# Gathering the table rows of a graph attention layer by item, straight into place, instead of by tile through a ring

## What is computed

```python
k = _decomp(node_feat, node_type, w_comp_k, w_basis_k).reshape(n, H, DK)
q = _decomp(node_feat, node_type, w_comp_q, w_basis_q).reshape(n, H, DK)
v = _decomp(node_feat, node_type, w_comp_v, w_basis_v).reshape(n, H, DK)
kt = jnp.einsum('nhi,thij->tnhj', k, relation_att)[edge_type, src]
e = (q[dst] * kt).sum(-1) * relation_pri[edge_type] * scale
m = jax.ops.segment_max(e, dst, num_segments=n)
ex = jnp.exp(e - m[dst])
denom = jax.ops.segment_sum(ex, dst, num_segments=n)
a = ex / denom[dst]
vt = jnp.einsum('nhi,thij->tnhj', v, relation_msg)[edge_type, src]
agg = jax.ops.segment_sum(a[..., None] * vt, dst, num_segments=n)
out = _decomp(agg.reshape(n, DH), node_type, w_comp_a, w_basis_a)
out = jax.nn.relu(out + node_feat @ loop_weight + bias)
x = _layernorm(x + out)
```

## Time and profile before

| what | value |
|---|---|
| median of 3 runs | 1298.87 us (1296.42 to 1303.16) |
| the profiled execution: span from its first to its last instruction | 1757.2 us |
| its own time apart from the span | not recorded |
| mean granted TensorE clock | 0.783 of full |
| PE busy | 1160.7 us, 66% |
| DVE busy | 986.6 us, 56% |
| ACT busy | 785.6 us, 45% |
| POOL busy | 881.5 us, 50% |
| DMA, mean over the span | 176 GB/s |

### The profile page before, as it was taken

The page is one execution under the profiler, slowest core; times in us unless marked ns, Lnnn a source line. Parts: engine busy times, 40 slices in busy tenths (PEclk is TensorE's granted clock), DMA queues, the critical chain, the costliest instruction groups (busy, mean ns, idle before and its releaser), DMA issues.

```text
span 1757.2 us, 31429 instructions
## 1 busy us (share of the span) xinstructions
PE 1160.7 (66%) x6730; PEld 962.9 (55%) x6730; DVE 986.6 (56%) x2832; ACT 785.6 (45%) x2217; POOL 881.5 (50%) x915
## 2 busy tenths in 40 slices
PE   8989875657556565566566655566565666656698
PEld 5445434656545554455455554565455565545587
DVE  7877463555445555445555554455554566545677
ACT  4667454444434434443344343443444354434324
POOL 2775354555555554545454545455545554545233
PEclk9999997777677767876777667766777687777699
DMA  8878754555555555545455555555555555555675
GB/s 261 323 289 316 284 172 140 157 148 158 152 159 153 157 151 151 149 141 151 150 163 148 158 152 154 148 160 164 151 162 154 154 168 148 155 150 162 187 242 194
DMA packets 225149, 309.08 MB, mean 176 GB/s; under 512 B 32423, under 2 KB 191119, under 8 KB 217781
## 3 DMA queue, kind: packets, MB, share of 16 engines
q1 hardware_dynamic: 159996, 188.75, 30.6%
q0 software_dynamic: 38880, 106.25, 23.4%
q10 hardware_dynamic: 26088, 12.08, 2.4%
HBM read 139.52 MB, written 58.78 MB: 113 GB/s over the span
## 4 chain that ended last, share of the span: by engine, by line
SPq 34%; issue 31%; PE 12%; DVE 9%; another core or an unknown queue 7%; DMA 2%; DVEq 2%; ACT 1%; POOL 1%; POOLq 0%; ACTq 0%
SPq L1173 27%; PE pb L1900 4%; SPq L1152 2%; PE pb L1923 2%; DVE agg L845 2%; SPq L481 2%; SPq L1170 2%; DVEq L814 2%; DMA kv<-ring 2%; PE pb L2084 1%; SPq L1168 1%; PE pb L2190 1%; PE pb L2028 1%; DVE kv L541 1%
## 5 line engine op out<-in xcount | busy, mean ns | idle before, releaser
L1458 POOL DMA_INDIRECT ring<-table,rows_idx x782 | 745.8, 954 | 736.6 <-SPq L1168 452.5
L2084 PE MATMUL pb<-work,onehot 128*128 128x136 f32 x1664 | 367.5, 358 | 214.1 <-DVE agg L845 152.8
L845 DVE TENSOR_TENSOR agg<-agg,pb 128x136 f32 x832 | 241.8, 291 | 459.9 <-remote 291.8
L2084 PEld LDWEIGHTS pb<-work,onehot 128*128 128x128 f32 x1664 | 307.0, 254 | 242.0 <-issue 210.9
L1650 ACT ACTIVATE work<-pb 128x512 f32<-128x512 f32 x208 | 124.0, 596 | 549.6 <-remote 376.2
L2028 PE MATMUL pb<-q_all,work 128*128 x1664 | 301.0, 340 | 1.3 <-issue 0.8
L2028 PEld LDWEIGHTS pb<-q_all,work 128*128 128x128 f32 x1664 | 280.6, 253 | 7.6 <-issue 4.9
L1637 ACT ACTIVATE work<-lane,neg_lane 128x128 f32<-128x128 f32 x800 | 253.3, 390 | 0.6
L2012 PE MATMUL pb<-ident,onehot 128*128 128x128 f32 x832 | 174.5, 347 | 115.6 <-issue 60.2
L2012 PEld LDWEIGHTS pb<-ident,onehot 128*128 128x128 f32 x832 | 125.4, 180 | 136.0 <-issue 71.3
L686 DVE TENSOR_TENSOR kv<-kv,pb 128x512 f32<-128x512 f32 x208 | 141.5, 680 | 96.6 <-issue 41.7
(11 more groups left out here) (239 smaller groups left out, 1237.2 us busy)
## 6 DMA issues: line engine op xcount, KB each, us to landing
kv<-ring SPq DMA_DIRECT2D x832, 128.0 KB
table<-kv SPq DMA_DIRECT2D x49, 1024.0 KB, 5.2
ring<-table,rows_idx POOLq DMA_INDIRECT x782
kv<-base_rows SPq DMA_DIRECT2D x7, 448.0 KB, 7.6
kv<-in_x_dram SPq DMA_DIRECT2D x8, 384.0 KB, 5.8
seg<-item_bias ACTq DMA_DIRECT2D x48, 64.0 KB
base_rows<-pair ACTq DMA_DIRECT2D x24, 128.0 KB
onehot<-coef_rows SPq DMA_DIRECT2D x3, 1024.0 KB, 5.5
```

The costliest lines, as they stand in the source:

```text
L845: v.tensor_tensor(a, a, PB[banks[i // 2 % len(banks)]][:, (i % 2) * 256:(i % 2) * 256 + W], ALU.add).then_inc(s_added, 1)
L1458: pool.indirect_dma_start(out=ring[:, o:o + 2 * D], out_offset=None, in_=table, in_offset=bass.IndirectOffsetOnAxis(ap=rows_idx[:, t:t + 1 ...
L2084: mm = t_.matmul(PB[banks[k % len(banks)]][:, u * 256:u * 256 + W], onehot[:, o:o + P], wv[:, b % WR, h * 2 + u, :], start=True, stop=True)
```

## The change

The row numbers are laid out by item. They are made early on GpSimd, between the pair products of the set-up, stored by tile in a new DRAM tensor `tile_src`, and gathered by item (seven small indirect DMAs, 512 B rows). TensorE and VectorE then turn and copy 128 columns instead of 112; the last two turns stand at blocks 38 and 39 instead of 37 and 38. `rows_idx` has a column for each item.

In the groups GpSimd alone brings the rows: for each batch it waits until the batch two groups back is weighted and until the batch two before has landed, and issues four gathers from `table` straight into `kv`, 832 in all. The ring, its counts, the 832 copies by SyncE, the tile numbers in `itile` and GpSimd's register loads are gone. SyncE keeps its loads and stores of stages one and three. A smaller buffer `spare` serves stage three where the ring did.

```diff
@@ GpSimd, set-up @@
             for k in range(IPR):
                 did(g_.tensor_scalar(pair[:, 0:TILES], tstart, item_no[:, k:k + 1], None, ALU.is_le))
                 g_.tensor_tensor(pair[:, TILES:2 * TILES], pair[:, 0:TILES], tgap, ALU.mult)\
                     .then_inc(s_pair_made, 1)
+                if k == 1:
+                    pool.wait_ge(s_tile_more, 16 * 4)
+                    did(g_.tensor_copy(srcf, tsrc))
+                if k == 3:
+                    did(g_.tensor_copy(etf, tedge))
+                if k == 5:
+                    did(g_.tensor_scalar(srcf, srcf, float(T), None, ALU.mult))
+            did(g_.tensor_tensor(srcf, srcf, etf, ALU.add))
+            pool.dma_start(tile_src.rearrange("(p c) e -> p c e", c=TPR), srcf.rearrange("p (c e) -> p c e", c=TPR))\
+                .then_inc(s_tile_src, 16)
...
-            pool.wait_ge(s_tile_more, 16 * 4)
-            did(g_.tensor_copy(srcf, tsrc))
-            did(g_.tensor_copy(etf, tedge))
-            did(g_.tensor_scalar(srcf, srcf, float(T), None, ALU.mult))
-            g_.tensor_tensor(srcf, srcf, etf, ALU.add).then_inc(s_lanes_rows, 1)
+            pool.wait_ge(s_tile_src, 16)
             pool.wait_ge(s_item_keys, 32)
             pool.dma_start(krow, item_keys.rearrange("(a k) i -> a k i", a=1)).then_inc(s_item_keys, 16)
+            for k in range(IPR):
+                pool.indirect_dma_start(
+                    out=item_src[:, k, :], out_offset=None, in_=tile_src,
+                    in_offset=bass.IndirectOffsetOnAxis(ap=ic[:, 0, k:k + 1], axis=0)).then_inc(s_item_src, 16)
@@ GpSimd, groups @@
-            def landed(t):
-                pool.wait_ge(s_tile[t % TSEMS], t // TSEMS * 16 + 16)
-                pool.sem_inc(s_landed, 1)
-
-            for t in range(REAL):
-                if t >= AHEAD:
-                    landed(t - AHEAD)
-                if t >= RING and t % 2 == 0:
-                    (done,) = nc.values_load_multi_w_load_instructions(
-                        next_start[0:1, t + 1 - RING:t + 2 - RING], engines=(pool.engine,), min_val=1,
-                        max_val=GROUPS * G, skip_runtime_bounds_check_because="counted from tiles")[1]
-                    pool.wait_ge(s_freed, done & 1023)
-                    hold_apart(pool)
-                o = t % RING * 2 * D
-                pool.indirect_dma_start(
-                    out=ring[:, o:o + 2 * D], out_offset=None, in_=table,
-                    in_offset=bass.IndirectOffsetOnAxis(ap=rows_idx[:, t:t + 1], axis=0))\
-                    .then_inc(s_tile[t % TSEMS], 16)
-            for t in range(REAL - AHEAD, REAL):
-                landed(t)
+            def bring(n):
+
+                g, b = n // NBATCH, n % NBATCH
+                par = g % 2
+                after(pool, s_weighted, g - 2, NBATCH, b + 1)
+                if n >= 2:
+                    pool.wait_ge(s_gathered[(n - 2) // NBATCH % 2][(n - 2) % NBATCH],
+                                 (n - 2) // (2 * NBATCH) * 64 + 64)
+                for u in range(4):
+                    o = (par * G + b * 4 + u) * 2 * D
+                    pool.indirect_dma_start(
+                        out=kv[:, o:o + 2 * D], out_offset=None, in_=table,
+                        in_offset=bass.IndirectOffsetOnAxis(
+                            ap=rows_idx[:, 4 * n + u:4 * n + u + 1], axis=0))\
+                        .then_inc(s_gathered[par][b], 16)
+
+            for n in range(GROUPS * NBATCH):
+                bring(n)
@@ SyncE: `bring` and its loops go, the two loads of stage three stay @@
+            sp.wait_ge(s_weighted, (GROUPS - 2) * NBATCH + 4)
+            sp.wait_ge(s_base_stored, 16 * (GROUPS - 4))
+            load_base(0)
+            sp.wait_ge(s_item_sums, (GROUPS - 2) * 2 * NBATCH + HALF * NB // 2)
+            load_coefs(0, 0, HALF)
```

More of the change, by code:

```diff
@@ L86, in graph_transformer_layer @@
     WORK = 4 * P + 2 * 4 * P + WR * 4 * W + 2 * IH * P + 3 * IH * P
[L88 to L92, removed]
+    assert GROUPS * G < ITEMS
     table = nc.dram_tensor("table", [NP * T, 2 * D], f32, kind="Internal").ap()
@@ L129, in graph_transformer_layer @@
         neg_lane = sb("neg_lane", [P, ITEMS])
-        rows_idx = sb("rows_idx", [P, TILES], i32)
-        strip = sb("strip", [97, ITEMS])
+        rows_idx = sb("rows_idx", [P, ITEMS], i32)
+        strip = sb("strip", [33, ITEMS])
         carries = strip[0:1, :]
[L135 to L138, removed]
+        iblk = strip[32:33, :].bitcast(i32)
         band = sb("band", [33, 3 * ITEMS // 2])
@@ L144, in graph_transformer_layer @@
         kv = sb("kv", [P, 2 * G * 2 * D])
-        ring = sb("ring", [P, RING * 2 * D])
+        spare = sb("spare", [P, CN + 4 * NB * P])
         onehot = sb("onehot", [P, 2 * G * P])
@@ L217, in graph_transformer_layer @@
         tsrc, tedge = [a0.take(TPR * P, TROWS).bitcast(i32) for _ in range(2)]
+        srcf, etf = [a0.take(TPR * P, TROWS) for _ in range(2)]
         a0.at = at
@@ L242, in graph_transformer_layer @@
         y = [s3.take(CN) for _ in range(2)]
-        yo = (s3.take(CN), ring[:, 0:CN])
+        yo = (s3.take(CN), spare[:, 0:CN])
         an = [s3.take(CN) for _ in range(2)]
@@ L258, in graph_transformer_layer @@
         even_coefs = take_coefs(q3, CB)
-        ring_coefs = take_coefs(Space(ring, RING * 2 * D, at=CN), HALF)
+        spare_coefs = take_coefs(Space(spare, CN + 4 * NB * P, at=CN), HALF)
         first_coefs, odd_coefs = take_coefs(h3, HALF), take_coefs(h3, HALF)
@@ L291, in graph_transformer_layer @@
         s_item_starts = sem("s_item_starts")
-        s_lanes_rows = sem("s_lanes_rows")
+        s_lanes = sem("s_lanes")
+        s_tile_src = sem("s_tile_src")
+        s_item_src = sem("s_item_src")
         s_stage0 = sem("s_stage0")
@@ L320, in graph_transformer_layer @@
         s_q_terms = sem("s_q_terms")
-        s_tile = [sem(f"s_tile{r}") for r in range(TSEMS)]
-        s_landed = sem("s_landed")
-        s_freed = sem("s_freed")
         s_segments = [sem(f"s_segments{r}") for r in range(2)]
@@ L426, in coef_of @@
             if ch == 1 and c0 < HALF:
-                return ring_coefs[:, c0:c1, :, :]
+                return spare_coefs[:, c0:c1, :, :]
             if ch % 2:
@@ L1149, in _ @@
                         .then_inc(s_segments[g], 16)
[L1151 to L1178, removed]
             def load_base(ch):
@@ L1877, in turn_items @@
                 if i == 0:
-                    pe.wait_ge(s_lanes_rows, 1)
+                    pe.wait_ge(s_lanes, IPR)
+                if i == 2:
+                    pe.wait_ge(s_item_src, 16 * IPR)
                 bank_free()
-                many = (P, TROWS)[a]
-                each = (lanes, srcf.rearrange("p (c e) -> p c e", c=TPR))[a]
+                each = (lanes, item_src)[a]
                 for k in range(k0, k1):
-                    t_.transpose(PB[0][:, (k - k0) * P:(k - k0) * P + many], each[:, k, :],
-                                 ident[0:many, 0:many]).then_inc(s_items_turned, 1)
+                    t_.transpose(PB[0][:, (k - k0) * P:(k - k0 + 1) * P], each[:, k, :],
+                                 ident[:, :]).then_inc(s_items_turned, 1)
                 bank0.append((s_items_copied, a * IPR + k1))
@@ L1997, in _ @@
             query_products(CHUNKS - 1, 0)
-            pe.wait_ge(s_item_blocks, 48)
+            pe.wait_ge(s_item_blocks, 32)
             L = IH * P
```

21 lines of the change are left out of this document (8 added, 13 removed).

## The result

| | before | after |
|---|---|---|
| median, us (lowest to highest, runs) | 1300.06 (1296.42 to 1303.16, 4) | 1334.51 (1333.71 to 1336.44, 4) |
| ratio after/before, 95% interval | | 1.0269 (1.0240 to 1.0299) |
| forecast | | 1357 (1325 to 1380) |

Slower, as forecast, and inside the range, but 22 us faster than the number.

The account below looks back on a forecast made before the run. The prediction took GpSimd's gathers to bound the groups, with SyncE's copies beside them. It summed 1298.9 + 62.7 for 50 more gathers − 4.5 for the copies = 1357 us, range 1325 to 1380.

Parts of the forecast that it names:

- The freezes: Profile of before: stretches where engines stood still, 452.5 us of GpSimd waiting for SyncE, taken to belong to the recording alone.
- 782 become 832 … +62.7: GpSimd's gathers: 50 more, since tiles spanning blocks are gathered per item, at 1.254 us spacing, +62.7 us, all on the path.
- GpSimd's gathers bound the groups, and SyncE's copies run beside them: Groups of before: 5.0 us a batch for gathering against 4.1 for SyncE's copies, which were taken as hidden.
- Copies … −4.5 us: SyncE's 832 copies go; all but those of the last tiles were taken as hidden behind gathers: −4.5 us.
- The 17.7 missing … I carry them over: Remainder of 1281.2 us summed against 1298.9, put down to time around the span and a start hold in both kernels.
- Start: GpSimd's first wait for weighting against the old hold at the coefficient rows: −0.4, taken as 0, bounded by −10 and +10.
- New waits on GpSimd: Waits for batch n−2 landed and batch n−16 weighted: nothing in the steady state.
- Compute: Compute in the groups needs 4.1 us a batch against 5.0 for gathering, so it follows the gathers closely.
- Landing: A gather's rows land at most 3.4 us after it ends; the new wait allows 6.3 us from its start.
- the late-landing rival: Scattered 1 KB rows land later than 6.3 us after their gather's start; with 7.3 us, +103, 1460 us; chance 0.04.
- The first: Rival: gathers really cost 0.954 us, the ring's hand-over between SyncE and GpSimd bound before; 1230 us after; chance 0.10.
- The second: Rival: compute bound the kernel before at 4.43 us a batch, so the time stays at 1299 us; chance 0.06.

Follow-up runs that it names:

- experiment 4: The kernel after with 52 more gathers into a spare buffer, one behind every fourth batch: 1397.98 us, ratio 1.0719.
- experiment 10: The kernel before with SyncE's wait for the batch before's landing ahead of its second copy instead of its third: 1448.96 us, ratio 1.1085.
- experiment 1: The kernel before, unchanged, recorded a second time: span 1297.0 us, its own time 1299.16 us.
- experiment 9: The kernel before with SyncE's wait for the batch before's landing ahead of its fourth copy instead of its third: 1286.69 us, ratio 0.9848.
- experiment 2: The kernel before with SyncE bringing 16 batches instead of 12 before it stops for the coefficient rows: 1301.3 us, ratio 0.9986.
- experiment 7: The kernel after with only two of each batch's four gathers from the third group on, other places keeping stale rows: 1192.84 us, ratio 0.9142.
- experiment 3: The kernel before with a tile counted landed after four gathers instead of seven: 1350.33 us, ratio 1.0354.

## Why the prediction was right or wrong

**The freezes** belong to the recording: right, and shown now (1297.0 against 1757.2 us).

**"782 become 832 … +62.7"**: right. 50 × 1.2585 = 62.9, and 48 fewer and 52 more gathers moved the time by 1.21 and 1.22 us each, good to about 0.1. The 0.30 behind each gather is real time: by the busy 0.954 alone experiment 4 would have cost 49.6 us, not 63.5. The rule of the Trainium skill (Perfetto Trace Analysis, GPSIMD Engine Instruction), start-to-start spacing instead of the span, agrees with this kernel.

**"GpSimd's gathers bound the groups, and SyncE's copies run beside them"**: the first half held in the mean (4.72 of 4.75 us a batch), the second half failed. It priced SyncE by what it issues, 4.1 us a batch, and left out that L1168 waits in each batch for the landing of the batch before's last copy. With it the rounds shown are 4.52 to 5.39 us, about as long as four gathers, and experiment 10 shows that a longer round sets the time. The landings were in my rows, but as the price of the last tiles alone.

**"Copies … −4.5 us"**: mis-sized. What went with the ring was 5.7 us of holds in the gathers and 15.4 of the tail. Of the tail, 2.2 went with the moved wait (19.9 in experiment 1, 17.7 in experiment 9). The other 13.2 are 8.3 of the longer way through the ring and 6.4 of the shared tiles near the end, less 1.5 by which compute was slower after; how the 8.3 divide into round and count is not shown. I had priced none of it: I added a landing of 3.4 and the copies, 7.9 us in all, where 19.9 stood, and took compute to be ahead of the gathers up to the end.

**"The 17.7 missing … I carry them over"**: wrong, and the larger part of the miss. Only 1.7 to 2.2 us lie around the span and the start hold is nothing (experiment 2). A remainder of a sum that should close is a term not found; it was the round and the tail (8.0 of first to last gather and 12.0 of the tail over my terms, less 4.2 at the start), and most of it went with the change. That the result still lies in the range is partly luck: the lower end, 1325, let the 17.7 go together with a hold at the start, and experiment 2 shows no such hold.

**Start**: forecast 0 within 10. The first gather came 4.1 us earlier than in experiment 1; the recordings with the set-up of before have 194.1 to 196.4, those with the set-up of after 190.8 to 193.5, so about 3. The changed set-up was a small gain, which I had called nothing. Which of its steps gave it is not shown.

**New waits on GpSimd**: right. 4.0 us for weighted batches, 0.9 for landings. **Compute** 4.1 a batch: 4.16 in the mean, but 4.96 in the last group. **Landing** at most 3.4: 2.8 in the median, but 3.8 at most by the view of L1416 and 4.42 for the last gather. The 6.3 us that the wait allows were enough, and the late-landing rival is out. From the Trainium skill (DMA: Bandwidth & Descriptors, Anatomy of one DMA) the estimate was 2.3 us; the trace's 2.8 is counted from the issue's start.

**The sum again** with the measured terms, from 1297.0: +62.9 − 5.7 − 15.4 − 4.1 − 1.9 = 1332.8. Mine had −4.5 for the 21.1 of the second and third term.

**The rivals.** The first was half right: its "hand-over between SyncE and GpSimd" did hold before. It was wrong in tying that to a cheaper gather. The kernel had two bounds of about the same length, and I treated them as exclusive. The second, compute as the bound, is out: experiment 7 has it at 4.16 us a batch, not 4.43. I also expected a profiled span of 1350 to 1450; it was 1332.8.

## What to carry to other kernels

Price a queue by its round, that is its issues and the landing that it waits for before the next, and not by its issues alone. Moving one wait by one position is a test that costs one line, and here gave 1.5% by itself. When the sum of terms leaves a remainder, find it before it is carried over, above all if the change removes something of that kind. Where two engines hand over in turn, price both, since they can be equally near the bound, as here (4.72 and 4.75 us a batch): take one away and only the difference to the other comes free.

## What the runs showed of the hardware

The same program with the same instructions was recorded at 1757.2 us and at 1297.0, 35% longer, with SyncE's register instructions at 0.70 us in one place and 0.04 in another while other engines stood. What stretches one recording and not the next stays open; the span against the median of the runs tells it at once.

A copy between two buffers of the chip, 128 KB, landed 3.1 to 4.2 us after it was issued beside the gathers (experiment 1, between 1100 and 1128 us), in other places 2.5 to 4.8. A gather of the same size landed in 2.8 in the median with no copies, and at times only after about 5 us with them (experiment 3). GpSimd's gathers kept 1.2563 us with the copies (experiment 9) and 1.2585 without (after). The DMA share in the window 600 to 900 us (columns as in experiment 7) was 0.79 in experiment 1 and is 0.40 after, with the granted clock at 0.84 and 0.86. Of experiment 1:

```profile
600.00:900.00 300.00, 228.17 (x1481) 203.75 (x1480) 230.49 (x631) 185.88 (x558) 227.18 (x239) 0.84 0.79 228
```

and of the kernel after:

```profile
600.00:900.00 300.00, 214.55 (x1370) 191.49 (x1371) 217.03 (x598) 170.51 (x510) 227.40 (x238) 0.86 0.40 115
```

GpSimd is busy to 0.2 us the same in both, for 239 and 238 instructions, with half the traffic: in these two kernels what a gather takes of GpSimd does not depend on what moves beside it.
